# A decoder layer on one core: loads, value products and the tail put in another order, and two key tiles in a row in units 12 to 14

## The reference

```
x = x + self_attention(layernorm(x))          # 2 heads of 64, rotary positions, causal
x = x + cross_attention(layernorm(x), ctx)    # 16 heads of 8, 1601 keys, biases on q, k, v, o
x = x + ffn(layernorm(x))                     # 128 -> 512 -> 128, exact gelu

# cross attention
scores = einsum('bhqd,bhkd->bhqk', Q, K) / sqrt(8)
attn = softmax(scores);  ctx = einsum('bhqk,bhkd->bhqd', attn, V)
# ffn: the weights get a part that depends on tokens 1 to 16 of the same batch
h = gelu(x @ W1.T + scale * x @ m1.T + b1)
out = h @ W2.T + scale * h @ m2.T + b2
```

## Time and profile before

| | us |
|---|---|
| median of 3 runs | 362.56 (362.37 to 362.57) |
| the profiled execution's own time | 363.49 |
| its span in the profile | 361.7 |
| TensorE busy | 335.5 (93%) |
| VectorE busy | 296.9 (82%) |
| ScalarE busy | 293.5 (81%) |
| GpSimd busy | 132.8 (37%) |

### The profile page before, as it was taken

The page is one execution under the profiler, slowest core; times in us unless marked ns, Lnnn a source line. Parts: engine busy times, 40 slices in busy tenths (PEclk is TensorE's granted clock), DMA queues, the critical chain, the costliest instruction groups (busy, mean ns, idle before and its releaser), DMA issues.

```text
span 361.7 us, 12753 instructions
## 1 busy us (share of the span) xinstructions
PE 335.5 (93%) x5238; PEld 157.7 (44%) x5242; DVE 296.9 (82%) x608; ACT 293.5 (81%) x591; POOL 132.8 (37%) x213
## 2 busy tenths in 40 slices
PE   7789688999999998999999989999999999998987
PEld 3442233544546443644534435443344444342365
DVE  3979889699898997699999997999999989880043
ACT  1555169989898789998998888998889999999941
POOL 3230755398020203799520327337001335204010
PEclk9999889999999999999999999999999999999999
DMA  7544388031450222231352010203210102000011
GB/s 237 218 129 129 138 239 284 14 135 31 129 192 2 95 89 74 63 138 46 125 176 79 5 60 28 60 3 111 98 54 30 59 27 61 0 4 1 2 33 31
DMA packets 20217, 31.00 MB, mean 86 GB/s; under 512 B 1528, under 2 KB 17404, under 8 KB 20160
## 3 DMA queue, kind: packets, MB, share of 16 engines
q1 hardware_dynamic: 20160, 30.19, 26.0%
HBM read 18.84 MB, written 11.34 MB: 83 GB/s over the span
## 4 chain that ended last, share of the span: by engine, by line
PE 59%; ACT 12%; DVE 12%; issue 7%; DMA 5%; SPq 3%; POOL 2%; ACTq 0%; DVEq 0%; POOLq 0%
PE wsum L1198 20%; PE ring L1167 16%; PE ring L1213 12%; PE ring L1235 8%; ACT probs L1015 7%; DVE part_max L788 5%; DMA q_unit<-consts 3%; ACT q_unit L1025 2%; DMA k_rows<-k_parts 2%; ACT prob_self L1060 1%; DVE energy L851 1%; SPq L507 1%; SPq L559 1%; SPq L516 1%; PE ring L1241 1%
## 5 line engine op out<-in xcount | busy, mean ns | idle before, releaser
L788 DVE TENSOR_REDUCE part_max<-ring 128x1 f32<-128x512 f32 x384 | 237.1, 682 | 20.0 <-PE ring L1235 19.2
L1015 ACT ACTIVATE probs<-ring 128x512 f32<-128x512 f32 (+1 forms) x416 | 222.8, 599 | 24.2 <-PE ring L1213 20.4
L1198 PE MATMUL wsum<-probs,v_aug 128*32 128x256 f32 (+1 forms) x1664 | 132.6, 386 | 3.4 <-ACT unit_ctx L1019 3.2
L1213 PE MATMUL ring<-q_unit,k_unit 54*128 54x256 bf16 (+1 forms) x832 | 125.2, 273 | 2.4 <-ACT probs L1015 1.4
L1235 PE MATMUL ring<-k_unit,q_unit 54*128 54x512 bf16 x384 | 118.8, 386 | 9.1 <-ACT probs L1015 3.4
L1213 PEld LDWEIGHTS ring<-q_unit,k_unit 54*128 54x128 bf16 (+1 forms) x832 | 44.3, 96 | 94.4 <-issue 78.5
L1198 PEld LDWEIGHTS wsum<-probs,v_aug 128*32 128x32 f32 (+1 forms) x1664 | 39.7, 109 | 35.3 <-issue 28.7
L1235 PEld LDWEIGHTS ring<-k_unit,q_unit 54*128 54x128 bf16 x384 | 34.4, 93 | 22.4 <-ACT probs L1015 7.1
L615 POOL TENSOR_TENSOR max_parts<-neg_max,c_sb 128x8 bf16<-128x8 f32 x16 | 3.3, 208 | 96.5 <-DVE neg_max L796 96.5
L1025 ACT ACTIVATE q_unit<-ring 6x512 bf16<-6x512 bf16 x32 | 18.5, 580 | 4.5 <-PE ring L1250 4.3
L615 POOL TENSOR_TENSOR k_parts<-k_full,c_sb 128x802 bf16<-128x802 f32 x6 | 9.1, 1523 | 19.5 <-ACT k_full L1073 19.5
(11 more groups left out here) (141 smaller groups left out, 334.7 us busy)
## 6 DMA issues: line engine op xcount, KB each, us to landing
k_unit<-k_rows SPq DMA_DIRECT2D x30, 300.2 KB
ctx_sb<-ctx_t SPq DMA_DIRECT2D x3, 800.5 KB, 9.0
...
```

The source lines that it names most:

```text
L788: v_.tensor_reduce(part_max[:, par, q, head, hp, c:c + 1], ring[s][:, 0:MW], AX.X, ALU.max)\
L1015: a_.activation(probs[0:rows, i % PB, :], ring[s][0:rows, :], ACT.Exp).then_inc(drained[s], 1)
L1198: last = mm(wsum[32 * j:32 * j + 32, 0:S], v_aug[0:rows, v // UB % 3, at:at + 32], probs[0:rows, i % PB, S * (j // 2):S * (j // 2 + 1)], s ...
L1213: last = mm(ring[s][0:keys, S * hp:S * (hp + 1)], k_unit[rows, u, L * hp + P * t:L * hp + P * t + keys], q_unit[rows, u, hp, :], start=Tru ...
```

## The change

**Tables.** Batch 1's values: V0 goes to the start, between `qk` of batch 1 and the turn of unit 0's maxima; V1 goes to unit 0, tile 3; V2 and V3 stay in unit 3, at tiles 1 and 6 instead of 5 and 8. `U3` of batch 0 goes from ahead of the first maximum to behind the next key product. In the tail, `ln3` and one `o0` move ahead of `x3T`.

**Loads.** The zeros of units 1 to 3 are loaded at the very start. For batch 0 the queries of units 1 to 3 are loaded first, and their keys after that. For later batches the keys and zeros of the batch's first unit are issued ahead of the wait for the query split.

**Pairs.** In units 12, 13 and 14 tile 0 stands alone, and the tiles 1 and 2, 3 and 4, and so on to 11 and 12 are put together: scores and maxima of both, then the other work of both, then the sums of both.

```diff
-VALUES_AT = {(3, 0): "V0", (3, 2): "V1", (3, 5): "V2", (3, 8): "V3"}
+VALUES_AT = {(0, 3): "V1", (3, 1): "V2", (3, 6): "V3"}
...
-         ("pa1", 0), ("split", 0), ("U0", 0), ("U1", 0), ("pick0", 0), ("pb1", 0), ("pick1", 0), ("store1", 0), ("U2", 0), ("U3", 0), ("load", 0)]
+         ("pa1", 0), ("split", 0), ("U0", 0), ("U1", 0), ("pick0", 0), ("pb1", 0), ("pick1", 0), ("store1", 0), ("U2", 0), ("load", 0)]
...
-BETWEEN = ((("k10", 0), ("bo", 0)), (("k11", 0),), (("k20", 0),), (("k21", 0), ("K0", 1)), (("K1", 1), ("parts0", 1)),
+BETWEEN = ((("k10", 0), ("bo", 0), ("U3", 0)), (("k11", 0),), (("k20", 0),), (("k21", 0), ("K0", 1)), (("K1", 1), ("parts0", 1)),
...
-        ("post", "o0", 0), ("post", "Wo", 3), ("post", "o1", 0), ("post", "o0", 1), ("post", "o1", 1), ("post", "ln3", 3),
-        ("post", "x3T", 3), ("post", "low0", 3), ("post", "low1", 3), ("post", "low2", 3), ("post", "low3", 3),
-        ("post", "o0", 2), ("post", "g0", 3), ("post", "g1", 3), ("post", "g2", 3), ("post", "g3", 3), ("post", "o1", 2),
+        ("post", "o0", 0), ("post", "Wo", 3), ("post", "o1", 0), ("post", "o0", 1), ("post", "ln3", 3), ("post", "o1", 1),
+        ("post", "o0", 2), ("post", "x3T", 3), ("post", "low0", 3), ("post", "low1", 3), ("post", "low2", 3),
+        ("post", "low3", 3), ("post", "g0", 3), ("post", "g1", 3), ("post", "g2", 3), ("post", "g3", 3), ("post", "o1", 2),
...
+PAIRED = (12, 13, 14)
...
 def unit_plan(v):
...
-    plan = []
+    steps = []
     for t in range(KT):
+        plan = []
...
         plan += now
+        front, plan = plan, []
...
-        plan += sums
+        steps.append((front, plan, sums))
     assert not todo
-    return plan
+    together = [(0,)] + [(t, t + 1) for t in range(1, KT, 2)] if v in PAIRED else [(t,) for t in range(KT)]
+    return [item for tiles in together for part in range(3) for t in tiles for item in steps[t][part]]
...
-    plan += [("M", 1, 0), ("M", 1, 1), ("prep", "qk", 1), ("mT", 0), ("M", 1, 2), ("prep", "qks", 1)]
+    plan += [("M", 1, 0), ("M", 1, 1), ("prep", "qk", 1), ("prep", "V0", 1), ("mT", 0), ("M", 1, 2), ("prep", "qks", 1)]
...
+            def load_zeros(b, u):
+                for par in range(2):
+                    sp.dma_start(q_unit[HALF * par:HALF * par + MR, u, :, :].rearrange("p h n -> p (h n)").bitcast(F32),
+                                 consts[0:MR, C_COLS["zeros"][0]:C_COLS["zeros"][1]]).then_inc(unit_in[u], 16)
+
+            for u in range(1, UB):
+                load_zeros(0, u)
...
             def load_unit(b, u):
                 load_keys(b, u)
+                load_zeros(b, u)
                 load_queries(b, u)
 
             def load_rest(b):
                 for u in range(1, UB):
+                    load_queries(b, u)
+                for u in range(1, UB):
                     load_keys(b, u)
-                    load_queries(b, u)
...
                     elif name == "split":
+                        if b:
+                            load_keys(b, 0)
+                            load_zeros(b, 0)
                         sp.wait_ge(q_split, 4 * (b + 1))
...
                         if b:
-                            load_keys(b, 0)
                             load_queries(b, 0)
```

2 lines of the change are left out of this document (removed).

## The result

| | before | changed |
|---|---|---|
| median, us (19 runs each, side by side) | 362.19 (360.59 to 364.46) | 363.99 (362.02 to 366.92) |
| the profiled execution | 363.49, clock 0.991 | 362.02, clock 1.000 |

The ratio is 1.0054, 95% interval 1.0036 to 1.0071: slower by 0.5%, where 357.7 us and a gain of 1.3% had been forecast. The two profiled executions can mislead. That of the changed kernel is the shortest of its 19, 1.97 us under its median, and that of before is 1.30 over its own. The profiles differ by -1.47 us and the medians by +1.80.

A forecast was written before the change was run, and what follows sets the result against it. Bound by TensorE mid-kernel, no single engine in units 12 to 14, DMA waits at the start. -2.9 + 0.8 - 1.6 - 0.4 - 0.75 + 0.0 = -4.85 from 363.49 gave 358.6, median 357.7, range 355.2 to 361.4.

The forecast's parts named there:

- - 2.4 - 0.2: Start: gain in us from VectorE's idle time going (2.4) and the turn and what follows running at 2.4 GHz (0.2).
- Sum 0.0, between -1.6 and +1.8: Pairing in units 12 to 14: gains and losses cancel to 0.0 us, within that range.
- I take an idle time of under 1 us, so no fall of the clock: Start: TensorE waits under 1 us for unit 1's keys, so its granted clock does not fall.
- rival 2: Start: unit 1's keys land near 42, the clock falls, start +1.1 instead of -2.9, 361.7 us; chance 0.11.
- in at 40.3 to 41: Start: unit 1's keys, 615,000 bytes at 130 GB/s flowing from about 35.6, landed by 40.3 to 41 us.
- Rival 4: Start: keys of units 1 to 3 share six DMA engines evenly, +4.8 instead of -2.9, 365.4 us; chance 0.06.
- hidden: Start: V0's 1.08 us of TensorE costs nothing, as the turn of unit 0's maxima waits for GpSimd until 43.4.
- ScalarE has nothing until they are there: about 0.4 us: Turns into units 13 and 14: next scores wait for the later copy of the turned maxima, +0.8 us in all.
- ScalarE needs 7.75 / 14 = 0.554 us per exponential: Units 12 to 14: ScalarE needs 1.11 us per tile, so units 13 and 14 gain no more than ScalarE's gaps.
- Half of the changes go: TensorE wins 0.13 per tile: Pairs in units 12 to 14: half of TensorE's changes of kind vanish, saving it 0.13 us per tile.
- +0.05 for some 15 pairs: Pair loop, units 12 to 14: the eighth bank waits in a ring of seven, 2.26 us against 2.22, +0.7 in all.
- Rival 3: Units 12 to 14: pairing costs its full price (banks and turn), +1.8 instead of 0, 359.5 us; chance 0.20.

The follow-up runs named there:

- experiment 5: experiment 1 with batch 0's loads in the old order (keys, queries and zeros of a unit in turn): 360.31 us, ratio 0.9955 to before.
- experiment 1: The changed kernel without pairs, tiles of units 12 to 14 taken one by one again: 363.43 us, ratio 1.0008 to before.
- experiment 2: The kernel before with nothing but the pairs in units 12 to 14: 364.23 us, ratio 1.0068 to before.
- 6: experiment 5 with the zeros loaded at the very start: 360.38 us, ratio 0.9952 to before.
- 7: As 6, with key and query rows reordered so that a load uses eight DMA engines, not six: 360.32 us, ratio 0.9944.
- 10: As 6, with qk and V0 of batch 1 ahead of unit 1's first two maxima: 360.46 us, ratio 0.9936.
- 11: As 7, with qk and V0 of batch 1 ahead of unit 1's first two maxima: 360.43 us, ratio 0.9941.
- experiment 12: experiment 1 with SyncE waiting for unit 1's six loads before it issues weights and context: 360.67 us, ratio 0.9960.
- 17: As 10, with pairs in unit 15 alone: 359.06 us, ratio 0.9905 to before.
- experiment 8: The kernel before with pairs in units 12 to 14, but tiles 11 and 12 alone: one execution, 366.19 us; copy 11 to copy 14 50.47.
- 9: As experiment 8, with one of a pair's four maxima moved behind the pair's sums: one execution, 365.31 us; copy 11 to copy 14 51.45.
- experiment 3: experiment 1 with V0 of batch 1 back in unit 3, tile 0: 363.39 us, ratio 1.0028 to before.
- 16: The changed kernel, pairs too, with SyncE waiting for unit 1's six loads before it issues weights and context: 363.68 us, ratio 1.0011.
- 13: The kernel before with a ring of six PSUM banks instead of seven: one execution, 370.4 us; copy 11 to copy 14 50.25.
- 14: As experiment 8, with a ring of six PSUM banks instead of seven: one execution, 371.78 us; copy 11 to copy 14 52.49.

## Why the prediction was wrong

**Two steps failed.** By the ratios the new order of batch 0's loads costs 1.9 us (experiment 5 against 1), where "- 2.4 - 0.2" had been put down. The pairs cost 2.5 (1.7 by the changed kernel against experiment 1), where "Sum 0.0, between -1.6 and +1.8" stood. Together with -1.6 for all the rest (experiment 5) that is +2.8, or +2.0 with the smaller price of the pairs, against +1.80 measured; each term is uncertain by 0.6 to 1.3 us.

**Start, the gain of -2.4 was not there to be had.** The prediction took the start of the kernel before from one profile, in which the clock had fallen to 0.50. Both VectorE's idle time and the slow rope product are what that fall cost. In another execution of the same start code (experiment 2) the clock held, and the first exponential came at 46.13 instead of 48.67, 2.5 us sooner without any change. The turn was released there by VectorE's maxima and GpSimd's split, as it was in experiments 6, 7, 10, 11, 12 and 17, whose first exponentials come at 45.7 to 46.3. So the new order could save only the falls, in those executions that have one, and not 2.6 us of the median. Over all 122 executions of before beside the experiments, 57 had a mean clock of 0.991 or less, as this profile had. "I take an idle time of under 1 us, so no fall of the clock" failed in its first half: TensorE idled 1.92 us in the changed kernel's profile. That the clock held all the same was luck. After such a wait it falls in some executions and not in others, and rival 2 took the fall as certain.

**Start, the landing.** "in at 40.3 to 41" had its beginning right: the first packet of keys moved at 35.3 us ("from about 35.6"), and the six query loads ahead of them cost nothing, since their last packet ended at 35.4 in the changed kernel and before had its first packet of keys at 35.2. What it left out is the lag that its own rows show, of 41 by the bytes against 42.54 landed. In experiment 12 the 615,000 bytes were through at about 40.0 by the GB/s of the stretches, and the semaphore came at 41.18; with the wide loads held back the landings are 41.18, 41.6, 41.87 and 42.52. Rival 2 named this lag ("keys land near 42") with a chance of 0.11. Its landing came true; its start of +1.1 is that of experiment 1's profile (49.88 against 48.67), where the clock fell, and not that of the changed kernel's (46.88), where it held.

**Start, what moved besides.** The list of moved DMAs stopped at the keys. With the zeros gone and the queries issued in SyncE's waiting time, weights and context came 7.5 us sooner, onto the end of the keys' transfer, and by the ratios that is worth 1.7 us (1.0008 to 0.9960). Rival 4 had a slower start from sharing and named the wrong partner: the keys of units 2 and 3, for which no harm can be told (0.9960 against 0.9964). The Trainium skill, page "DMA: Bandwidth & Descriptors", section "Queues, rings and completion order", has each engine take the descriptors of a ring in order, and the runs agree for those keys. By that order alone the wide loads, behind the keys on the six engines, would be harmless too, and the runs say that they are not. They also run on the ten engines that the keys leave idle (share 0.93 to 1.01), and the packets of keys got slower while they did. What the two share no run here shows.

**Start, V0.** "hidden" rested on TensorE being free from about 42, and held where it was: in experiment 12 the keys landed at 41.18, V0 stood ahead of the turn, and the turn came at 43.45, at once behind GpSimd's split (43.40). In the changed kernel the maxima were late and V0 with them, and the turn came at 44.39, 0.84 behind the split.

**V1.** The table's +0.98 looks like the forecast +0.8 and does not confirm it. With V1 still in unit 3 the same stretch is 26.37 in before and 26.45, 26.81 and 27.20 in experiments 8, 9 and 2; with V1 in unit 0 it is 27.34 to 27.67 in all. Where the first exponential came early the difference is 0.15 to 0.5. The size lies somewhere between, and no run tested V1 by itself.

**V0 and V1 out of unit 3.** -1.73 for -1.6, of which V0 is 1.03 by experiment 3. Right, and by the reason given.

**Loads of units 4, 8 and 12.** "At unit 12 TensorE waited 0.78" is a row of one execution. The stretch to unit 11's copy is 0.36 shorter, for -0.4, but the pairs alone, with the loads of before, have it too (150.48), and TensorE's wait there was:

```profile
253.58 0.39 PE L1241 MATMUL ring<-k_unit,q_unit 54*128 54x512 bf16 x1 [0.24 <-DMA q_unit<-consts]
```

So the size came right by luck, by the choice of profile. What this edit is worth in the median lies between nothing and 0.3, and no run tested it by itself.

**Tail.** -1.04, where -0.75 between -0.5 and -0.9 stood: the mechanism was right and the size off. `g0` came 2.53 us after `x3T` (2.6 forecast, 3.45 before), so 0.92 is the moved `o0`; the 0.1 of delay that had been set against it did not come.

**Pairs, the late turn.** "ScalarE has nothing until they are there: about 0.4 us" saw the right place and priced one engine. It loses 0.52 and 0.24 at a turn, but TensorE 1.71 and VectorE 2.06, and in these units nobody has slack to make that up. It cost up to 1.36 (experiment 8, with the last pair of a unit in it) for +0.8, and in executions such as 16's a fall of the clock on top.

**Pairs, the loop.** "ScalarE needs 7.75 / 14 = 0.554 us per exponential", and so bounds units 13 and 14, was a wrong reading of the row. The row joins instructions with short idle times between them. One by one, the exponentials of the earlier trace rows start at 303.62, 304.11, 304.73, 305.22, 305.81, 306.30 and 306.95. Where the second's scores stood ready it started 0.49 us after the first; the next came 0.59 to 0.65 later, after up to 0.06 us without work. In rows of four the steps are 0.49, 0.48 and 0.48. So ScalarE can take one in 0.49 us and was waiting for TensorE's 1.11 per tile, briefly, in every tile. It was not the bound, and it had 0.13 us a tile to spare. "Half of the changes go: TensorE wins 0.13 per tile" is not borne out in size: six pairs of unit 15 gain 0.35 in all, 0.03 a tile.

What was put down as gained, the gaps behind the copy of the sums, is outweighed by new gaps behind the pairs. "+0.05 for some 15 pairs" priced these, and is the term that was mis-sized: as far as experiments 8, 13 and 14 show, the wait for the eighth bank was the right place, and it came out as 1.3 us instead of 0.7. The loop of a pair was put at 1.14 + 0.25 + 0.6 + 0.27 = 2.26. From tiles 5 and 6 to 7 and 8 of unit 12 in experiment 8, where no other work stands between, it takes 1.00 for the sums, 0.46 from their end to the first exponential, 0.60 for that, and 0.37 to the start of the next sums: 2.43. ScalarE has by then used up its four scores and idles. Rival 3 had the right sign and with +1.8 too low a top.

**The sum.** The sum -4.85 was set against one profiled execution. The changed kernel's own came 1.5 under that of before while the median rose by 1.8, so a single pair of profiles would have confirmed a gain.
